# Linear attention's channel means from a rounded and a remainder part, and GpSimd's products in pieces

## What is computed

```python
# 1: chunked linear attention with a gate (chunk of 32 tokens)
S = einsum(Q, K) * mask;  O = S @ V
x = layernorm(x + sigmoid(x @ W_g.T) * O @ W_o.T + x)
# 2: cross attention on ctx, 16 heads of 64, softmax over 512 keys
x = layernorm(x + xattn(x, ctx))
# 3: ternary feed-forward, 256 -> 1024 -> 256, squared relu, low-rank fast weights
x = layernorm(x + ffn(x))
# layernorm(x) = (x - mean) / sqrt(var + 1e-5), over the 256 channels
```

## Time and profile before

| | |
|---|---|
| median of 3 runs | 1275.75 us (1275.02 to 1280.24) |
| the profiled execution's own time | 1280.37 us |
| its span | 1278.2 us |
| TensorE busy | 1257.5 us (98%) |
| VectorE busy | 922.5 us (72%) |
| ScalarE busy | 797.9 us (62%) |
| GpSimd busy | 772.8 us (60%) |
| mean granted TensorE clock | 0.997 of full speed |

### The profile page before, as it was taken

One profiled execution on the slowest core, in us unless ns is written; L12 is line 12 of the kernel. 1 busy time (PEld: TensorE's weight loads), 2 busy tenths in 40 slices (PEclk: granted clock), 3 DMA queues, 4 the chain that ended last, 5 costly groups with the idle time before them and its releaser, 6 DMA issues.

```text
span 1278.2 us, 21163 instructions
## 1 busy us (share of the span) xinstructions
PE 1257.5 (98%) x6902; PEld 845.0 (66%) x6902; DVE 922.5 (72%) x1811; ACT 797.9 (62%) x1064; POOL 772.8 (60%) x445
## 2 busy tenths in 40 slices
PE   8899999999999999999999999999999999999997
PEld 6787865666566665756665666657566656677775
DVE  6788887666765668476657756684767677878887
ACT  3355456665665557465657565574656676778885
POOL 3633349986876779587858767785879587300000
PEclk9999999999999999999999999999999999999999
DMA  6311221001100110010011001100100110021101
GB/s 223 116 50 50 85 67 18 3 1 34 35 3 2 48 19 0 17 39 13 0 33 33 2 0 40 28 0 17 33 19 0 34 18 2 17 83 45 54 17 50
DMA packets 99424, 43.16 MB, mean 34 GB/s; under 512 B 77184, under 2 KB 82064, under 8 KB 99376
## 3 DMA queue, kind: packets, MB, share of 16 engines
q1 hardware_dynamic: 98560, 39.40, 12.4%
q0 software_dynamic: 816, 3.15, 0.8%
HBM read 29.66 MB, written 12.58 MB: 33 GB/s over the span
## 4 chain that ended last, share of the span: by engine, by line
PE 91%; DVE 3%; POOL 3%; issue 1%; DMA 1%; ACT 1%; SPq 0%; POOLq 0%; DVEq 0%; ACTq 0%
PE ps L1426 17%; PE ps L1401 15%; PE ps L48 12%; PE ps L50 11%; PE ps L49 10%; PE ps L1405 4%; PE ps L1417 4%; PE ps L1461 2%; PE ps L1463 2%; PE ps L1462 2%; PE ps L1438 2%; PE ps L1876 2%; PE ps L1877 2%; POOL acc L984 1%; DMA x_in<-in_xT 1%
## 5 line engine op out<-in xcount | busy, mean ns | idle before, releaser
L1217 DVE CUSTOM_DVE_ANT_0 junk<-ps,mask 128x512 bf16<-128x512 f32 x504 | 314.8, 687 | 87.7 <-PE ps L1417 86.4
L1071 ACT ACTIVATE prob<-ps,mcol 128x1024 f32<-128x1024 f32 x256 | 281.9, 1116 | 128.2 <-PE ps L1405 123.0
L984 POOL TENSOR_TENSOR acc<-acc,prob 128x1024 f32<-128x1024 f32 x126 | 300.5, 2385 | 11.5 <-POOL acc L981 0.4
L981 POOL TENSOR_TENSOR acc<-prob 128x1024 f32<-128x1024 f32 x63 | 150.5, 2389 | 193.6 <-ACT prob L1071 192.6
L1426 PE MATMUL ps<-prob,v_b 128*64 128x512 f32 x1024 | 244.5, 598 | 0.0
L998 POOL TENSOR_TENSOR acc_lo<-acc,acc_hi 128x1024 f16<-128x1024 f32 x63 | 136.4, 2165 | 5.1
L1426 PEld LDWEIGHTS ps<-prob,v_b 128*64 128x64 f32 x1024 | 67.8, 136 | 107.2 <-issue 73.8
L1401 PE MATMUL ps<-q_hi,k_hi 64*128 64x512 f32 x512 | 113.9, 441 | 0.2
L1405 PE MATMUL ps<-shift,ones_r 64*128 64x512 f32 x512 | 101.3, 391 | 0.1
L1401 PE MATMUL ps<-q_lo,k_hi 64*128 64x512 f32 x512 | 101.2, 391 | 0.0
L1401 PE MATMUL ps<-q_hi,k_lo 64*128 64x512 f32 x512 | 101.1, 391 | 0.0
(11 more groups left out here) (265 smaller groups left out, 2940.1 us busy)
## 6 DMA issues: line engine op xcount, KB each, us to landing
shift<-nmx SPq DMA_DIRECT2D x512, 0.5 KB, 2.0
x_in<-in_xT SPq DMA_DIRECT2D x8, 512.0 KB, 3.8
x_scratch<-x_a SPq DMA_DIRECT2D x8, 512.0 KB, 2.9
raw<-in_cT SPq DMA_DIRECT2D x8, 512.0 KB, 3.7
raw<-x_scratch SPq DMA_DIRECT2D x8, 512.0 KB, 3.9
y<-x_scratch SPq DMA_DIRECT2D x8, 512.0 KB, 3.7
y_scratch<-y SPq DMA_DIRECT2D x8, 512.0 KB, 2.8
outT<-x SPq DMA_DIRECT2D x7, 512.0 KB, 2.7
```

What stands on the lines that cost most here:

```text
L981: pool.tensor_tensor(total, prob[:, 0], prob[:, 1], ALU.add).then_inc(acc_out, 1)
L984: pool.tensor_tensor(total, total, prob[:, kt], ALU.add).then_inc(acc_out, 1)
L1071: act.activation(prob[:, i].rearrange("p h t -> p (h t)"), banks.rearrange("p h t -> p (h t)"), ACT.Exp, scale=SCALE, bias=mcol[:, i:i + 1 ...
L1217: dve.tensor_tensor_reduce(junk[:, t % 2, h], SMAX[t % 2][:, h], mask[:], -1.0, -LOWEST, ALU.add, ALU.min, nmx[:, p % 2, t, h:h + 1]).then ...
```

## The change

1. **Sums in two parts.** For batches 0 to 6, mean and variance are two fp32r matmuls (`sum_parts`): `mean_r` times `sum_hi` (the sum rounded, by ScalarE: `mean_hi`, `variance_hi`) plus `mean_r` times `sum_lo` (the remainder, by VectorE: `mean_lo`, `variance_lo`). Batch 7 keeps the float32 matmul. `sum_hi` and `sum_lo` lie over `sq`.
2. **Places.** On TensorE the variance of b-2 moves behind the queries, and the mean behind all values. On VectorE the comparisons move behind `split_gated`. The variance of batch 6 moves behind the first queries of the second phase.
3. **Rounding of the gated output.** From batch 1 on ScalarE makes `og_hi` (`round_gated`); VectorE keeps the remainder.
4. **GpSimd.** The products are made in pieces of 256 columns, the splits of `x_lo` and `c_lo` in two halves, and the staging DMAs of Wk and Wv wait until x of batch 2 and of batch 3 has landed.

```diff
@@ the buffers
+        c["mean_r"] = sb(whole, "mean_w", [P, P], F32R)
+        c["mean_w"] = f32(c["mean_r"][:])
...
-    sq = sb(ctx, "sq_a", [P, DK, T], F32)
+    with ExitStack() as squares:
+        sq = sb(squares, "sq_a", [P, DK, T], F32)
+    sum_hi, sum_lo = (sb(ctx, n, [P, T], F32R) for n in ("sum_hi_a", "sum_lo_a"))
@@ gpsimd
             if i:
                 pool.wait_ge(stage_split, 2 * CHUNKS * i)
+                pool.wait_ge(x_in[(i + 1) % 2], 32)
...
+        PIECES = [slice(j * D, j * D + D) for j in range(HID // D)]
+        done = 0
         for k in range(DK):
...
+            for cols in PIECES:
+                pool.tensor_tensor(wfc[:, k, cols], sign[:, k, cols], wfc[:, k, cols], ALU.mult).then_inc(f_step, 1)
+                pool.wait_ge(f_step, done + 1)
+                pool.tensor_tensor(wfc[:, k, cols], wfc[:, k, cols], scale[:, cols], ALU.mult).then_inc(f_step, 1)
+                pool.wait_ge(f_step, done + 2)
+                pool.wait_ge(f_low, k + 1)
+                pool.tensor_tensor(c["wfc"][:, k, cols], c["wfc"][:, k, cols], wfc[:, k, cols],
+                                   ALU.add).then_inc(f_step, 1)
+                done += 3
...
-            pool.tensor_tensor(c["tern"][:, rows], c["tern"][:, rows], wpr[:, rows], ALU.mult).then_inc(f_step, 1)
+            for row in range(k * HK // DK, (k + 1) * HK // DK):
+                pool.tensor_tensor(c["tern"][:, row], c["tern"][:, row], wpr[:, row], ALU.mult).then_inc(f_step, 1)
...
-            pool.tensor_tensor(c_lo[:], raw_c, f32(c_hi[:]), ALU.subtract).then_inc(c_split, 1)
+            for k in range(DK):
+                op = pool.tensor_tensor(c_lo[:, k], raw_c[:, k], f32(c_hi[:, k]), ALU.subtract)
+            op.then_inc(c_split, 1)
@@ scalar
+        def round_gated(b):
+            act.wait_ge(gate_used, b + 1)
+            act.wait_ge(y_ps, 2 * b)
+            act.activation(og_hi[:], og[:], ACT.Copy).then_inc(og_rounded, 1)
+
+        def variance_hi(b):
+            act.wait_ge(sq_sum_out, b + 1)
+            act.activation(sum_hi[:], tile_sum[:], ACT.Copy).then_inc(var_hi_out, 1)
+
+        def mean_hi(b):
+            act.wait_ge(y_sum_out, b + 1)
+            if b > 0:
+                act.wait_ge(var_ps, b)
+            act.activation(sum_hi[:], tile_sum[:], ACT.Copy).then_inc(mean_hi_out, 1)
...
         for b in range(2, B):
             front(b)
             query_copies(b)
             deviation(b - 2)
+            mean_hi(b - 1)
             values(b)
             square(b - 1)
+            variance_hi(b - 1)
+            round_gated(b)
             if b in (3, 4):
                 low_rank(b - 3)
@@ vector
+        def mean_lo(b):
+            dve.wait_ge(mean_hi_out, b + 1)
+            dve.tensor_tensor(sum_lo[:], tile_sum[:], f32(sum_hi[:]), ALU.subtract).then_inc(mean_lo_out, 1)
+
+        def variance_lo(b):
+            dve.wait_ge(var_hi_out, b + 1)
+            dve.tensor_tensor(sum_lo[:], tile_sum[:], f32(sum_hi[:]), ALU.subtract).then_inc(var_lo_out, 1)
...
             if b > 1:
                 root(b - 2)
+            mean_lo(b - 1)
             mask_scores(b)
...
             gated(b)
             sum_squares(b - 1)
+            variance_lo(b - 1)
+            split_gated(b)
             if b in (3, 4):
                 compare_in(b - 3)
             if b in (5, 6):
                 compare_out(b - 5)
-            split_gated(b)
@@ tensor
+        def sum_parts():
+            pe.matmul(ST, c["mean_r"][:], sum_hi[:], start=True, stop=False)
+            return pe.matmul(ST, c["mean_r"][:], sum_lo[:], start=False, stop=True)
...
         def step(b, par):
             gates(b, par)
+            queries(b, par)
             if b > 1:
                 variance(b - 2)
-            queries(b, par)
...
             outputs(b - 1)
             scores(b, par)
-            values(b, par, (0, 1))
-            if b == B - 1:
-                values(b, par, (2, 3))
+            values(b, par, (0, 1, 2, 3))
             if b == 1:
                 pe.wait_ge(f_mid, 2)
             mean(b - 1)
-            if b < B - 1:
-                values(b, par, (2, 3))
             attend(b)
```

More of the change, by code:

```diff
@@ L87, in decoder_layer @@
         c = {}
-        c["mean_w"] = sb(whole, "mean_w", [P, P], F32)
+        c["mean_r"] = sb(whole, "mean_w", [P, P], F32R)
+        c["mean_w"] = f32(c["mean_r"][:])
         c["ones_w"] = sb(whole, "ones_w", [P, P], F32)
@@ L337, in linear_attention_phase @@
     f_sign, f_above, f_step = sem("f_sign"), sem("f_above"), sem("f_step")
+    og_rounded, var_hi_out, var_lo_out, mean_hi_out, mean_lo_out = (
+        sem(n) for n in ("og_rounded", "var_hi_out", "var_lo_out", "mean_hi_out", "mean_lo_out"))
     STAGED, CHUNKS = ("Wq", "Wk", "Wv"), 2 * DK
@@ L408, in _ @@
                                    ALU.subtract).then_inc(stage_split, 1)
+        PIECES = [slice(j * D, j * D + D) for j in range(HID // D)]
+        done = 0
         for k in range(DK):
-            n = 3 * k
             pool.wait_ge(f_sign, 1)
             pool.wait_ge(f_above, k + 1)
[L414 to L419, removed]
+            for cols in PIECES:
[7 more added lines that the diff above has]
+                done += 3
         for k in range(DK):
-            rows = slice(k * HK // DK, (k + 1) * HK // DK)
             pool.wait_ge(f_sign, 2)
             pool.wait_ge(f_above, DK + k + 1)
-            pool.tensor_tensor(c["tern"][:, rows], c["tern"][:, rows], wpr[:, rows], ALU.mult).then_inc(f_step, 1)
+            for row in range(k * HK // DK, (k + 1) * HK // DK):
+                pool.tensor_tensor(c["tern"][:, row], c["tern"][:, row], wpr[:, row], ALU.mult).then_inc(f_step, 1)
     @block.scalar
@@ L486, in _ @@
         act.activation(wpr[:], wpr[:], ACT.Abs).then_inc(f_abs, 1)
+        mean_hi(0)
         values(1)
         square(0)
+        variance_hi(0)
+        round_gated(1)
         for b in range(2, B):
@@ L604, in split_gated @@
         def split_gated(b):
[L605 to L610, removed]
+            if b == 0:
+                dve.wait_ge(gate_used, 1)
+                dve.tensor_copy(og_hi[:], og[:]).then_inc(og_split, 1)
+                dve.wait_ge(og_split, 1)
+            else:
+                dve.wait_ge(og_rounded, b)
+            dve.tensor_tensor(og_lo[:], og[:], f32(og_hi[:]), ALU.subtract).then_inc(og_split, 1 if b == 0 else 2)
         def scales():
@@ L707, in gates @@
             mm.then_inc(g_ps, 1)
+        def sum_parts():
+            pe.matmul(ST, c["mean_r"][:], sum_hi[:], start=True, stop=False)
+            return pe.matmul(ST, c["mean_r"][:], sum_lo[:], start=False, stop=True)
         def mean(b):
-            pe.wait_ge(y_sum_out, b + 1)
-            if not (isinstance(b, int) and b == 0):
+            if b > 0:
                 pe.wait_ge(rs_out, 2 * b - 1)
-            pe.matmul(ST, c["mean_w"][:], tile_sum[:], start=True, stop=True).then_inc(mean_ps, 1)
-        def variance(b):
-            pe.wait_ge(sq_sum_out, b + 1)
-            pe.matmul(ST, c["mean_w"][:], tile_sum[:], start=True, stop=True).then_inc(var_ps, 1)
+            if b < B - 1:
+                pe.wait_ge(mean_lo_out, b + 1)
+                sum_parts().then_inc(mean_ps, 1)
+            else:
+                pe.wait_ge(y_sum_out, b + 1)
+                pe.matmul(ST, c["mean_w"][:], tile_sum[:], start=True, stop=True).then_inc(mean_ps, 1)
+        def variance(b):
+            if b < B - 1:
+                pe.wait_ge(var_lo_out, b + 1)
+                sum_parts().then_inc(var_ps, 1)
+            else:
+                pe.wait_ge(sq_sum_out, b + 1)
+                pe.matmul(ST, c["mean_w"][:], tile_sum[:], start=True, stop=True).then_inc(var_ps, 1)
         def values(b, par, tiles):
@@ L957, in batch @@
                     next_masks(b + 1)
-        sp.wait_ge(la.f_step, 3 * DK + DK)
+        sp.wait_ge(la.f_step, 3 * DK * HID // D + HK)
         load_masks(0)
@@ L1001, in split_x @@
             pool.wait_ge(x_rounded, b + 1)
-            pool.tensor_tensor(x_lo[:], raw_x, f32(x_hi[:]), ALU.subtract).then_inc(x_split, 1)
+            for k in range(DK):
+                op = pool.tensor_tensor(x_lo[:, k], raw_x[:, k], f32(x_hi[:, k]), ALU.subtract)
+            op.then_inc(x_split, 1)
         def split_c(b):
             pool.wait_ge(c_rounded, b + 1)
-            pool.tensor_tensor(c_lo[:], raw_c, f32(c_hi[:]), ALU.subtract).then_inc(c_split, 1)
+            for k in range(DK):
+                op = pool.tensor_tensor(c_lo[:, k], raw_c[:, k], f32(c_hi[:, k]), ALU.subtract)
+            op.then_inc(c_split, 1)
         def centre_output_weight(half):
@@ L1165, in _ @@
         act.wait_ge(la.vec_in, 16 * 5)
-        act.wait_ge(la.f_step, 3 * DK + DK)
+        act.wait_ge(la.f_step, 3 * DK * HID // D + HK)
         for g in range(2):
@@ L1555, in _ @@
             keys(0, g, g, FIRST_KEY[g])
-        la.variance_late()
         pe.wait_ge(la.s_out, B)
         queries(0, 0, 0, FIRST_QUERY[0])
```

(1 more changed line is left out.)

## The result

The changed kernel takes **1280.10 us** in the median of 20 executions (1279.41 to 1281.58), the kernel before 1275.05 in the median of 20 beside it (1273.99 to 1280.24). The ratio is 1.0038 with a 95% interval of 1.0032 to 1.0044: about 5 us slower, where 1.25 us faster was forecast. The time lies in the range of 1265 to 1281 and within 0.5% of the kernel before, but on the other side of it.

A forecast was written before the change was run, and what follows sets the result against it. TensorE bounds the first phase before the change, the ScalarE and VectorE loop after it. First phase -1.85, variance of batch 6 -0.4, second phase +1.0: -1.25 from 1275.75 gives 1274.5 us, range 1265 to 1281.

The forecast's parts named there:

- 3.8 + 1.7 of gain: Before and in step 2: starting 3.8 us earlier as x lands sooner, plus 1.7 us of work lost to the half clock.
- -0.4 and +1.0: Behind the first phase: variance of batch 6 saves 0.4 us; GpSimd's split halves cost the second phase 1.0.
- the second rival: In steps 4 and 5, new TensorE gaps halve the clock: four falls at 1.7 us, time 1282, chance 0.10.
- The loop of ScalarE and VectorE: Within one first-phase step, second query copy to next batch's query copies: 17.1 us against TensorE's 15.8, becoming the bound.
- GpSimd's pieces: In steps 4 and 5, 256-column products hold up five VectorE instructions: 1.5 us in all.
- Step 3: A first-phase step of the batch loop, filled by TensorE: no loss from the change, 16.9 us.
- The start: Beginning of step 2, after TensorE ends step 1: at 39.5 us instead of 43.31.
- The second phase: At seven batch ends, splitting x_lo and c_lo in halves on GpSimd costs 0 to 1.7 us, taken as 1.0.
- The clock rival: In steps 4 and 5, waits of 1.5 to 2 us lower TensorE's clock: 1.7 us a fall, 1282, chance 0.10.
- The first rival: In the first phase TensorE stays the bound: phase ends at 138.95, time 1263, or 1269 with half; chance 0.24.
- The third: Before step 2, the x load stays as slow as before: start at 42.1, time 1278.8, chance 0.08.
- The drain at a table switch: On ScalarE, 1.38 us of drain per switch: two pauses in four steps, 11 us, time 1285.5, chance 0.01.

The follow-up runs named there:

- before_wait: The kernel before with only the two waits of the staging DMAs for x of batches 2 and 3: 1275.39 us, ratio 0.9996.
- the float32 sums: The changed kernel with all means and variances as one float32 matmul again, at their new places: 1274.57 us, ratio 0.9990.
- after_nowait: The changed kernel without the two waits of the staging DMAs: 1281.22 us, ratio 1.0045.
- after_whole_splits: The changed kernel with x_lo and c_lo split in one instruction each, as before: 1282.30 us, ratio 1.0047.
- after_whole_products: The changed kernel with GpSimd's products of the ternary weights whole, as before: 1279.15 us, ratio 1.0021.
- before_again: The kernel before, unedited, profiled once more: median 1275.45 us, ratio 0.9998; the profiled execution 1275.40 us, span 1273.3.
- f32_all_whole: The changed kernel with float32 sums, whole GpSimd products, and x_lo and c_lo split in one instruction each: 1273.94 us, ratio 0.9986.
- f32_whole_products: The changed kernel with float32 sums and whole GpSimd products: 1275.40 us, ratio 0.9994.
- after_round_vector: The changed kernel with the gated output rounded on VectorE again: 1281.50 us, ratio 1.0041.
- after_f32_variance: The changed kernel with float32 variances, the means still in two parts: 1276.51 us, ratio 1.0009.

## Why the prediction was wrong

**The step that failed** is the last of the sum: "It lies 4.6 above the median of the runs, at their upper end; the difference carries over". It did not carry over, because the 4.6 us were the very stall that the change was credited with removing: 3.2 of waiting before step 2 and the half clock behind it, for which the prediction took 1.7 and the two profiles show 1.4. The second profile of the kernel before has neither, and before_wait shows them worth nothing in the median. Two numbers in the text, 4.6 above the median and 3.8 + 1.7 of gain in one place, were the same thing counted once as noise and once as a gain. Taken against the usual execution, the prediction's own end of the first phase (149.25 against 145.62, 3.6) with its -0.4 and +1.0 gives +4.2, and with the median of 1275.05 a time of 1279.3.

That the two profiled spans came out 0.7 us apart, near the forecast of 1.25, is in part luck: the steps below miss by up to 1.5 us either way, so that the first phase ended 1.05 earlier than said, and what follows cost 1.0 more. In the second rival 1282 lies 6.3 above the median, inside the 6.4 that the prediction called no change, though its chance was counted outside.

**Point by point**, predicted and measured, in us:

| | predicted | measured |
|---|---|---|
| x of batch 2 lands, after its issue | 3.8 | 3.6 |
| step 2 starts | 39.5 | 37.99 |
| step 2 | 19.45 | 19.06 |
| step 3 | 16.9 | 18.04 |
| step 4 | 19.6 | 19.10 |
| step 5 | 19.6 | 19.72 |
| step 6 | 17.1 | 16.92 |
| step 7 | 17.1 | 17.37 |
| first phase ends | 149.25 | 148.20 |
| the rest, variance included | +0.6 | +1.6 |

- *The loop of ScalarE and VectorE* was right, in mechanism and in size: 16.92 to 17.37 where 17.1 was the sum of its terms, and the waits stood where they were named. That this loop is what costs the time, the float32 sums show.
- *GpSimd's pieces*: 1.5 was taken for five instructions; in step 5 four of them lost 1.8 and the fifth, `x1`, nothing.
- *Step 3* was mis-sized by 1.1. I gave it no loss. VectorE's `scales`, for which TensorE's outputs of step 3 wait through `f_scale`, stands behind `og_lo`, which took 2.30 us beside GpSimd's splitting; so `pscale` ended at 64.12 and TensorE stood 0.96. In after_nowait, after_whole_splits and after_whole_products, whose step 3 is written the same, that wait was 0.5 to 0.6 and the step took 17.63 to 17.66; so 0.7 of the 1.1 comes each time, and 0.4 came in this execution.
- *The start* came 1.5 early: batch 0's work ended sooner (step 1 began at 22.85, for 24.27), which differs from execution to execution (22.85 to 24.27 in these profiles), and step 1 needed 15.14.
- *The second phase* cost 1.4 by the two traces, from the first keys to the last (925.63 us against 924.20 in before_again), and the third 0.2. Of the 1.4, 0.7 is the late `og_lo` at the seam, which I had not priced: TensorE waits 0.82 for it, with only the first queries ahead. The other 0.7 fits the halves, which were priced at 1.0: f32_all_whole, which has none, gains 0.96 over seven batch ends on f32_whole_products, 0.14 each.
- *The clock rival*: in the changed kernel's profile the clock stayed at 1.00 behind waits of 1.32 and 1.88. In after_whole_splits it stayed behind one of 1.88 as well. In after_nowait, after_round_vector and after_f32_variance it fell behind waits of 1.88, 1.83 and 1.88, and step 6 took 17.63, 17.66 and 18.07 where the changed kernel has 16.92. So it is real, in three of these five profiles, once an execution and not four times, and at 0.7 to 1.2 us rather than 1.7.
- *The first rival*, TensorE as the bound, is excluded by 8.1 us of idle time. *The third*, x as slow as before, was the wrong question: x is slow only when its issue comes second.
- *The drain at a table switch*: the sigmoid starts 1.29 behind its table load, as in the earlier trace rows, and the loop closes without it. The Trainium skill's 1.38 (ScalarE: Activation LUTs, What ACT_TABLE_LOAD costs) shows in no run here.

**Where the 4.2 us between the spans of 1273.3 and 1277.5 are**: the start of step 2 gives 1.24; step 2 gives 0.21, step 3 takes 0.37, step 4 1.41, step 5 3.20, step 6 gives 1.00, step 7 takes 0.05; the seam takes 0.68, the rest of the second phase 0.75, the third 0.2. That the medians differ by some 5 and the spans by 4.2 may lie in falls of the clock that this profile happens not to have: of the changed kernel's 20 executions the four slowest (1281.16 to 1281.58 us) all have a mean clock of 0.996, the three at 0.998 took 1279.41 to 1280.19, and the profiled one had 0.997. None of the slow ones was profiled, so that is argued, not shown. Why the first gates sometimes take 2.8 us and sometimes up to 4.9 was not tried either. It does not decide the race for x by itself: they took 4.8 in the first profile and 4.1 in after_nowait, where x was issued 0.58 ahead of Wk and landed in 3.4.

The largest single loss, step 5, shows what TensorE's saving was worth where it did not bind: it did 16.46 us of work in 19.72.

## What to carry to other kernels

Before a stall in a profile is priced as a gain, hold the profiled execution against the median: if it lies above by about as much as the stall is long, profile again, since the usual execution may not have it. An engine that is 98% busy does not make its cheaper instruction a gain when the saving is bought with instructions on two engines whose common loop already takes 14 of its 16.5 us; add up that loop first, with hand-overs, and compare it to the step. Undo the parts one at a time: here one part cost more than the whole loss, and with it, the pieces and the halves gone the rest is 1.6 to 1.8 us under the kernel before.

## What the hardware showed

- A 512 KB load issued 0.44 us after a 1 MB load from another queue took 6.5 us to land; issued 0.55 us before it, 3.5. The two executions lie 5 us apart.
- Behind waits of the same length, 1.88 us, the granted clock fell in two profiles (0.56 and 0.50 over some 2 us) and stayed at 1.00 in two others.
- VectorE's instructions with inputs from SBUF can take much longer beside GpSimd's: a 512-column remainder took 1.23 us instead of 0.69 beside 256-column pieces, a 1024-column one 2.30 instead of 1.23 beside the splitting of Wv, a 512-column root 2.35 instead of 0.69 beside a whole split. Not each does (`x1` kept its 1.21 us), and GpSimd's grow as well: a product of 256 columns took 1.71 us instead of 0.74.
